# An attention kernel on eight cores: the softmax normalization of a query block moved behind the scores of the next block

## The reference

```python
logits = jnp.einsum('bhqd,bhkd->bhqk', q, k) / SCALE
logits = logits - alpha[:, None, None] * dist[None]      # dist = |i - j|
attn = jax.nn.softmax(logits, axis=-1)
out = jnp.einsum('bhqk,bhkd->bhqd', attn, v)
out = out.transpose(0, 2, 1, 3).reshape(B, T, D)
out = out @ out_w.T + out_b
...
g = _silu(_L0_ffn_ref(xn, L0_ffn_w_up, L0_ffn_w_down))
x = x + s * g
```

## Time and profile before

| | us |
|---|---|
| median of 3 runs | 5781.39 |
| lowest and highest of them | 5765.88, 5896.3 |
| the profiled execution | 5768.78 |
| its span on the slowest core, core 2 | 5767.2 |
| spans of the 8 cores | 5749.8 to 5767.2 |

### The profile page before, as it was taken

The page is one execution under the profiler, slowest core; times in us unless marked ns, Lnnn a source line. Parts: engine busy times, 40 slices in busy tenths (PEclk is TensorE's granted clock), DMA queues, the critical chain, the costliest instruction groups (busy, mean ns, idle before and its releaser), DMA issues.

```text
span 5767.2 us, 41821 instructions; the slowest of 8 cores (5749.8 to 5767.2 us)
## 1 busy us (share of the span) xinstructions
PE 3796.1 (66%) x14494; PEld 1252.7 (22%) x14646; DVE 1071.5 (19%) x1461; ACT 1179.0 (20%) x1425; POOL 311.2 (5%) x581
## 2 busy tenths in 40 slices
PE   4077675875766767747677577285656566657777
PEld 0023221211221221212122122031212121213333
DVE  1611111111111112222212221110111111111111
ACT  1100231331322213313323232100222222210000
POOL 0000000000000000000000000000111111110000
PEclk9588787887877887868888788687888898988898
DMA  1000110110110001101111110122000000023232
GB/s 59 7 26 8 31 39 26 37 38 21 41 30 23 5 7 51 58 19 55 48 34 55 36 40 4 55 64 91 31 27 31 27 31 28 31 77 108 102 110 97
DMA packets 85734, 246.33 MB, mean 43 GB/s; under 512 B 16990, under 2 KB 17022, under 8 KB 83606
## 3 DMA queue, kind: packets, MB, share of 16 engines
q1 hardware_dynamic: 56886, 167.82, 9.3%
q0 software_dynamic: 28640, 75.82, 3.9%
HBM read 167.79 MB, written 75.50 MB: 42 GB/s over the span
## 4 chain that ended last, share of the span: by engine, by line
PE 64%; DMA 12%; DVE 10%; ACT 7%; issue 7%; ACTq 0%; DVEq 0%; POOLq 0%; SPq 0%; POOL 0%
PE ps L768 17%; PE ps L969 5%; PE ps L967 5%; PE ps L1060 4%; PE ps L1058 4%; PE ps L736 3%; PE ps L755 3%; DMA attn_scr<-pt 2%; PE ps L992 2%; PE ps L534 2%; PE ps L536 2%; PE ps L738 2%; PE ps L737 2%; PE ps L532 2%; DVE pt L827 2%
## 5 line engine op out<-in xcount | busy, mean ns | idle before, releaser
L768 PE MATMUL ps<-pt,v_hat 128*65 128x512 f32 x2048 | 979.4, 625 | 0.0
L797 ACT ACTIVATE pt<-ps,negc 128x2048 f32<-128x2048 f32 x256 | 503.7, 1968 | 1117.3 <-PE ps L755 742.3
L969 PE MATMUL ps<-xn_lo,wt_up 128*128 128x512 bf16 x1024 | 456.7, 446 | 32.8 <-DMA wt_up<-wup_t_scr 26.1
L736 PE MATMUL ps<-q_hi,k_hi 64*128 64x512 bf16 x1024 | 220.0, 425 | 351.1 <-ACT pt L797 344.8
L967 PE MATMUL ps<-xn_hi,wt_up 128*128 128x512 bf16 x978 | 439.2, 449 | 2.0 <-ACT rfb L957 2.0
L1058 PE MATMUL ps<-h_ahi,wt_dn 128*128 128x512 bf16 x982 | 376.7, 384 | 84.2 <-DMA h_alo<-h_scr_lo 84.2
L1060 PE MATMUL ps<-h_alo,wt_dn 128*128 128x512 bf16 x1024 | 392.8, 384 | 54.0 <-DMA h_alo<-h_scr_lo 51.7
L992 PE MATMUL ps<-h2b,ones_row 128*1 128x512 f32 x256 | 137.3, 618 | 402.4 <-ACT h2b L989 402.4
L768 PEld LDWEIGHTS ps<-pt,v_hat 128*65 128x65 f32 x2048 | 275.6, 144 | 561.8 <-issue 561.8
L978 ACT ACTIVATE hful<-hpre 128x512 f32<-128x512 f32 x128 | 80.7, 630 | 825.5 <-DVE hpre L974 825.5
L974 DVE TENSOR_TENSOR hpre<-ps,rfb 128x512 f32<-128x512 f32 x128 | 88.6, 692 | 778.8 <-PE ps L969 778.8
(11 more groups left out here) (218 smaller groups left out, 3767.1 us busy)
## 6 DMA issues: line engine op xcount, KB each, us to landing
wstg<-wup_in SPq DMA_DIRECT2D x128, 256.0 KB, 2.8
wstg<-wdn_in SPq DMA_DIRECT2D x128, 256.0 KB, 2.8
h_scr_hi<-hhi POOLq DMA_DIRECT2D x128, 128.0 KB, 2.0
h_scr_lo<-hlo POOLq DMA_DIRECT2D x128, 128.0 KB, 2.0
h_ahi<-h_scr_hi SPq DMA_DIRECT2D x4, 4096.0 KB
h_alo<-h_scr_lo SPq DMA_DIRECT2D x4, 4096.0 KB
attn_scr<-pt POOLq DMA_DIRECT2D x64, 128.0 KB, 2.2
wup_t_scr<-wtout POOLq DMA_DIRECT2D x64, 128.0 KB, 2.0
```

The lines of the kernel that those rows point to most:

```text
L736: out_list.append(lambda: c.inc(te.matmul(pb, kh, qh, start=True, stop=False), "sc_mm0"))
L768: c.inc(te.matmul(ps[0:65, b * 512:(b + 1) * 512], vrr[:, kc, h, 0:65], ptb[:, pcol:pcol + 512], start=(kc == 0), stop=(kc == KC - 1)), "p ...
L797: c.inc(sc.activation(ptb, ps[0:128, 0:2048], AF.Exp, bias=negc[:, 0:1]), "exp")
L969: c.inc(te.matmul(ps[0:128, b * 512:(b + 1) * 512], wt, xl, start=False, stop=(dc == DC - 1)), "up_mm" if dc == DC - 1 else "up_mm0")
```

## The change

The norm of a block is put into a function `emit_norm(qb)` with the same instructions and waits. It is no longer called at the end of its block, but in the next block of the same pair, at group 0, behind the scores' matmuls and ahead of that group's exp. The norm of the last block of a pair is called behind the loop. Nothing else is changed.

```diff
+        def emit_norm(qb):
             c.wait(sc, "pv_g", c.val("pv_g"))
             c.wait(sc, "nb_a", c.val("nb_a"))
             c.wait(sc, "nb_b", c.val("nb_b"))
             c.inc(sc.activation(pt1[64:65, 0:512], ...), "nr_a")
             c.inc(sc.activation(pt1[64:65, 512:1024], ...), "nr_b")
...
             drain_w(2)
+
+        pending_norm = None
+        for qb in range(QB):
+            pending = None
+            for kcg in range(KCG):
...
+                for i in range(max(len(mmsA), len(mmsB))):
+                    if i < len(mmsA):
+                        mmsA[i]()
+                    if i < len(mmsB):
+                        mmsB[i]()
+                if kcg == 0 and pending_norm is not None:
+                    emit_norm(pending_norm)
+                    pending_norm = None
+                if pending is not None:
+                    emit_pv(*pending)
+                c.wait(sc, "sc_mm")
...
+                c.wait(sc, "d_at", c.val("d_at"))
+                c.inc(sc.activation(ptb, ps[0:128, 0:2048], AF.Exp, bias=negc[:, 0:1]), "exp")
...
+            emit_pv(*pending)
+            pending_norm = qb
             if stop_after == f"P{p}q{qb}":
                 break
+        if pending_norm is not None:
+            emit_norm(pending_norm)
+            pending_norm = None
```

More of the change, by code:

```diff
@@ L838, in build_program @@
             drain_w(2)
+        pending_norm = None
+        for qb in range(QB):
+            pending = None
+            for kcg in range(KCG):
+                kc0, kc1 = 2 * kcg, 2 * kcg + 1
+                ptb = pt0 if kcg % 2 == 0 else pt1
+                c.wait(te, "exp", c.val("exp"))
+                mmsA, mmsB = [], []
+                score_mms(hA, qb, kc0, 0, mmsA)
+                score_mms(hA, qb, kc1, 1, mmsA)
+                score_mms(hB, qb, kc0, 2, mmsB)
+                score_mms(hB, qb, kc1, 3, mmsB)
+                for i in range(max(len(mmsA), len(mmsB))):
[9 more added lines that the diff above has]
+                c.wait(sc, "sc_mm")
+                c.wait(sc, "c_cp")
+                c.wait(sc, "pv_g", max(0, c.val("pv_g") - 1))
+                c.wait(sc, "at_b", c.val("at_b"))
+                c.wait(sc, "nc_b", c.val("nc_b"))
+                c.wait(sc, "d_at", c.val("d_at"))
+                c.inc(sc.activation(ptb, ps[0:128, 0:2048], AF.Exp, bias=negc[:, 0:1]), "exp")
+                for (h, col, pcol) in ((hA, 0, 0), (hA, 1, 512), (hB, 0, 1024), (hB, 1, 1536)):
+                    kc = 2 * kcg + col
+                    if kc * 128 >= qb * 512 and (kc + 1) * 128 <= (qb + 1) * 512:
+                        off = pcol + (kc * 128 - qb * 512)
+                        c.wait(ve, "exp")
+                        c.inc(ve.tensor_mul(ptb[:, off:off + 128], ptb[:, off:off + 128],
+                                            e2diag[:, (0 if h == hA else 128):(128 if h == hA else 256)]),
+                              "pt_fix")
+                pending = (ptb, kc0, kc1)
+                drain_w(2 if p < NP // 2 else 3)
+            emit_pv(*pending)
+            pending_norm = qb
             if stop_after == f"P{p}q{qb}":
                 break
+        if pending_norm is not None:
+            emit_norm(pending_norm)
+            pending_norm = None
         if stop_after is not None and stop_after.startswith(f"P{p}"):
```

## The result

| | before | after |
|---|---|---|
| lowest run, us | 5765.9 | 5823.7 |
| median of 17 runs each, us | 5834.4 | 5867.2 |
| ratio | 1 | 1.0111, 95% interval 1.0072 to 1.0150 |
| span of core 2 in the profiled execution, us | 5767.2 | 5820.0 |
| first to last scores (the attention stage), core 2, us | 2964.0 | 3030.1 |

The change makes the kernel 1.1% slower. Some executions of every kernel here show a lower granted clock on a whole die, or on both, and take longer: the medians contain them, the ratios leave them out, and the stages in the tables are read from cores without it. I compare core 2 with core 2.

The account below looks back on a forecast made before the run. It took the chain from PV's end through norm and DMAs to the next exp, 17.50 us at 24 block changes, as the bound; 5768.8 + 24 x 2.34 (56.2), clock zero, gave 5825 us, range 5795 to 5865.

Parts of the forecast that it names:

- within 2%: Whole kernel: the time changes by no more than 2% either way, 90%; slower by more 8%, faster by more 2%.
- Only TensorE's order changes; the exp's waits still include the norm: At 24 block changes the exp still waits for products, reciprocals and DMAs; nothing of the 17.50 us comes off its front.
- The copies wait for the scores through the shared count: Copies of the sums wait on a semaphore shared with the scores, so they start only when the moved scores are complete.
- The first rival: Copies don't wait for the scores; the chain moves 0.5 us a place, 12 us in all, 5781 us; chance 3%.
- 2.34 us a place: At each of 24 block changes the copy starts 2.55 us after PV instead of 0.21, 56 us more in all.
- The broadcasts keep the high clock: The norm's broadcast matmuls were costed at the high clock, 587 to 610 ns each, so no time was added.
- the second rival: Low clock from the moved scores on: scores 1.7 us and broadcasts 1.8 us slower a place, 5909 us; chance 8%.
- The stretch to the third scores: zero, 12 us either way: From second to third scores after a block change: no net clock effect, bounds 12 us less or more.
- The long gap doesn't keep the clock: TensorE's idle gap before the second scores grows from 12.6 to 16.1 us; these again start at the low clock.
- the third rival: The high clock lasts through the gap: 80 us less against 56 more, 5745 us; chance 3%.
- How the numbers follow: Prediction's part setting chances and range: 12 us either side for clock, as much again for run spread, range 5795 to 5865.
- the forecast's own: The case of +2.34 us at 24 places with nothing for the clock, 5825 us; chance 84%.

Follow-up runs that it names:

- own_sem: The changed kernel with the two broadcasts counted on a semaphore of their own, so the copies don't wait for the moved scores; attention stage 2966.4 us, lowest time 5766.0.
- delay_only: The kernel before, in its old order, with ten extra matmuls between last PV and norm that the copies wait for; attention stage 3013.8 us, lowest time 5820.8.
- warm_bc2: The changed kernel with six extra matmuls between the moved scores and the broadcasts, second run; attention stage 3002.2 us, lowest time 5801.9.
- fill_gap2: The changed kernel with 36 extra matmuls behind the norm's first reciprocal, second run; attention stage 2963.0 us, ratio to the kernel before 1.0019.
- flat2: Against the kernel before: scores before last PV, norm beside next block, own semaphores for fixes and exps, weight work moved; stage 2502.2 us, lowest time 5298.0.

## Why the prediction was right and wrong

Right: the sign, the place and the mechanism of the main term, the copies' wait. Wrong: one term of the sum, the clock of the broadcasts, and the spread of runs in the range. The forecast was +56 us on 5768.8, a ratio of 1.0097, with "within 2%" at 90%; measured is 1.0111 (1.0072 to 1.0150), and on core 2 +53 in the span and +66 in the stage. That the span's +53 lies so near to 56 is partly luck: the 24 places grew by 70.5 us, and 13 us less in stages that the change does not touch, with 4 less in the rest of the attention, hid the error. In the order of the steps:

- *Only TensorE's order changes; the exp's waits still include the norm.* Right. All 24 exps are released by the transfer as before (396.3 us, in the groups by line above; the prediction had "near 375", which ignored the slower broadcasts).
- *The copies wait for the scores through the shared count.* Right, and shown by own_sem (without it +2 us) and delay_only (with the delay alone +50). The first rival is out by the releaser of 24 copies.
- *2.34 us a place.* 2.12 measured, 50.9 us in sum against 56.2 (the copies' idle time grew from 132.7 to 183.8 us, about 189 foretold). The step took the time from the scores' start to an exp, 2.62 us; a copy starts 2.40 us after the scores' start. An instruction of the same kind, as the copy itself 0.21 us behind PV, would have been the nearer row. Why the exp starts later than the copy was not tried.
- *The broadcasts keep the high clock.* Wrong: +22.2 us where zero was put. This is the step of the sum that failed. The argument was that a longer stretch of dense work and a gap of the same size come before them. That is so, but at all 24 places the clock was down by the last broadcast instruction, where before it fell only in the first scores behind them, and there the delay was free. Why it falls just there stays open; warm_bc2 shows only that six more matmuls ahead of them prevent it. The price of the full case stood in the second rival (1.8 us a place); half of it came true (0.92 us a place), while the scores themselves stayed at full clock.
- *The stretch to the third scores: zero, 12 us either way.* Right, -1.7 us. TensorE's idle time ahead of the scores: about 417 us foretold, 414.7 found.
- *The long gap doesn't keep the clock.* Right, the third rival is out: the second scores still last 0.61 us an instruction pair. With the same gap filled (fill_gap2) the stretch behind it takes 56 us less.

The range failed too. 5795 to 5865 was laid around the time of one execution, with the spread of two runs, while the stated time is a median over all, 5867.2 us, 2 us above the range. The step that failed is the one in "How the numbers follow" that took the spread of the runs as 15.5 us and passed over the third run shown, 5896.3: the median before has itself moved from 5781.4 to 5834.4 us with 14 more runs. On that baseline the forecast would have been 5891, 23 us too high, so the small miss of the range says little about the sum.

Of the cases named, the forecast's own came true with a part of the second rival in it.

## What to carry to other kernels

Where tags share one semaphore, moving instructions changes what every wait on the current count waits for: check each wait on the moved queue's count, not only its own data. Here one such wait was the whole loss (+66 us with it, +2 us without), and another one cost 164 us in the kernel that was meant to mend it. Before moving work into an idle stretch, ask what ends the stretch: the scores could not shorten a wait that a buffer and a DMA ended, and freeing the buffer gave what the move could not.

## What the runs showed of the hardware that was not expected

TensorE's clock fell without any idle time. In flat2, core 4, the last PV of the block before (692.5), the scores (696.1), the one-row broadcasts (698.2), the next PV (700.1) and the scores behind it (705.4) follow each other without a gap. Three stretches of that timeline (columns as above):

```profile
696.10:698.20 2.10, 2.10 (x17) 0.60 (x16) 0.16 (x1) 1.63 (x3) 0.00 (x0) 1.00 0.00 0
698.20:700.00 1.80, 1.80 (x6) 0.45 (x4) 0.00 (x1) 1.46 (x1) 0.00 (x0) 1.00 0.44 127
700.10:705.30 5.20, 5.20 (x9) 1.39 (x8) 5.03 (x2) 0.41 (x1) 0.00 (x0) 0.67 0.02 6
```

The PV behind the broadcasts took 5.34 us instead of 3.65, at a clock of 0.67, though TensorE was busy throughout. So a stretch without idle time is no promise of the full clock. It is no rule either: on this core the PV at this spot was slow at 4 of the 24 places and took 3.65 us at the other 20, behind the same kinds of TensorE instructions. What decides between them was not tried.
